# Causal attention with one key head: another order of the query tiles, and part of the second half of the queries computed behind the first shift

## The reference

```python
q = (x @ wq_w.T + wq_b).reshape(b, t, H, HD)        # H = 32, HD = 16, t = 1024
k = (x @ wk_w.T + wk_b).reshape(b, t, HKV, HD)      # HKV = 1
v = (x @ wv_w.T + wv_b).reshape(b, t, HKV, HD)
k1 = k[:, :, 0, :]
v1 = v[:, :, 0, :]
scores = jnp.einsum('bqhd,bkd->bhqk', q, k1) / jnp.sqrt(jnp.float32(HD))
causal = jnp.tril(jnp.ones((t, t), dtype=bool))
scores = jnp.where(causal, scores, -jnp.inf)
weights = jax.nn.softmax(scores, axis=-1)
attn = jnp.einsum('bhqk,bkd->bqhd', weights, v1)
attn = attn.reshape(b, t, H * HD)
return attn @ wo_w.T + wo_b
```

## Time and profile before

| | us |
|---|---|
| median of 3 runs (1402.65 to 1405.58) | 1404.99 |
| profiled execution, its own time | 1405.82 |
| its span, first to last instruction | 1403.9 |
| preparing of the first half of the queries and the keys | 820 to 854.8 |
| maxima of tile 7 with the late events | 854.8 to 905.4 |
| from the last of them to the first score | 905.4 to 911.8 |
| scores, to the last transposes | 911.8 to 1206.3 |

### The profile page before, as it was taken

How to read it: one execution, slowest core, us unless ns; L and a number is a source line. 1 busy time by engine, 2 the same in 40 slices (tenths; PEclk the granted TensorE clock), 3 DMA queues, 4 the chain that set the end, 5 groups by cost and what they waited for, 6 DMA issues and landing times. The chain is left out here.

```text
span 1403.9 us, 14513 instructions
## 1 busy us (share of the span) xinstructions
PE 1288.1 (92%) x5418; PEld 846.5 (60%) x5418; DVE 737.1 (53%) x1283; ACT 429.5 (31%) x718; POOL 162.9 (12%) x211
## 2 busy tenths in 40 slices
PE   7899999599799998987887989899999998799998
PEld 4788666244487787866665434355454443588776
DVE  4322432475666655335576746887776632433264
ACT  2121311211221124221222221166665665312141
POOL 0000000000086100003111240000010123000000
PEclk9999999799899999998898998999999999899999
DMA  8110000840155540005000010000000000122001
GB/s 321 46 45 0 0 0 0 335 152 0 67 203 202 202 179 0 1 0 171 0 1 0 1 45 0 2 0 3 2 2 2 2 3 1 46 82 75 0 23 38
DMA packets 18121, 79.07 MB, mean 56 GB/s; under 512 B 2960, under 2 KB 3600, under 8 KB 15888
## 3 DMA queue, kind: packets, MB, share of 16 engines
q1 hardware_dynamic: 18064, 78.32, 15.3%
HBM read 75.95 MB, written 2.10 MB: 56 GB/s over the span
## 5 line engine op out<-in xcount | busy, mean ns | idle before, releaser
L376 PE MATMUL psum<-L_ffn_x,L_ffn_w_up 128*128 128x512 f32 x1152 | 264.4, 391 | 3.5 <-DVE L_ffn_hidden L505 3.5
L376 PEld LDWEIGHTS psum<-L_ffn_x,L_ffn_w_up 128*128 128x128 f32 x1152 | 217.1, 189 | 50.5 <-DVE L_ffn_hidden L505 5.4
L1817 DVE TENSOR_REDUCE mqa_top<-psum 128x1 f32<-128x512 f32 (+3 forms) x304 | 186.2, 657 | 58.1 <-PE psum L1643 37.7
L1736 ACT ACTIVATE mqa_prob<-psum 128x512 f32<-128x512 f32 x288 | 159.9, 601 | 86.1 <-PE psum L1661 85.0
L393 PE MATMUL psum<-L_ffn_wd,L_ffn_part_h 128*128 128x512 f32 x600 | 142.7, 399 | 7.0 <-DVE L_ffn_wd L301 7.0
L1661 PE MATMUL psum<-mqa_stack,mqa_keys 100*128 100x512 f32 x288 | 133.0, 476 | 4.8 <-DMA mqa_stack<-mqa_rows 3.5
L393 PEld LDWEIGHTS psum<-L_ffn_wd,L_ffn_part_h 128*128 128x128 f32 x600 | 115.0, 193 | 31.9 <-DVE L_ffn_part_h L292 7.8
L1632 PE MATMUL psum<-mqa_keys,mqa_stack 96*128 96x512 f32 (+1 forms) x256 | 108.4, 445 | 1.9 <-DVE mqa_top L1817 1.0
L376 PE MATMUL psum<-L_attn_x,L_attn_w_up 128*128 128x512 f32 x456 | 105.4, 394 | 3.9 <-DVE L_attn_hidden L505 3.9
L376 PEld LDWEIGHTS psum<-L_attn_x,L_attn_w_up 128*128 128x128 f32 x456 | 86.7, 190 | 22.5 <-issue 4.3
L1661 PEld LDWEIGHTS psum<-mqa_stack,mqa_keys 100*128 100x128 f32 x288 | 55.3, 196 | 72.1 <-ACT mqa_prob L1736 62.6
(11 more groups left out here) (246 smaller groups left out, 1699.6 us busy)
## 6 DMA issues: line engine op xcount, KB each, us to landing
L_ffn_stage<-in_L_w SPq DMA_DIRECT2D x25, 768.0 KB, 6.2
L_ffn_z_int<-in_L_z SPq DMA_DIRECT2D x14, 768.0 KB, 4.4
L_ffn_s_all<-in_L_s SPq DMA_DIRECT2D x14, 768.0 KB, 6.2
lora_wo<-in_L_wo SPq DMA_DIRECT2D x8, 1024.0 KB, 9.6
L_attn_stage<-in_L_w SPq DMA_DIRECT2D x10, 512.0 KB, 3.7
L_attn_w_down<-in_L_down SPq DMA_DIRECT2D x1, 2560.0 KB, 24.4
x_feat<-in_x_feat SPq DMA_DIRECT2D x2, 1024.0 KB, 7.1
x_tok<-in_x_tok SPq DMA_DIRECT2D x1, 2048.0 KB, 18.8
```

The costliest lines, as they stand in the source:

```text
L376: ins = nc.tensor.matmul(bank[half][:, :], w_up[:, slot, w_part, at:at + P], x[:, x_part, k, half * HALF:(half + 1) * HALF], start=k == 0 ...
L1736: nc.scalar.activation(prob[:, n % PROBS, :], score_bank[n % 3], ACT.Exp, scale=SCALE)\
L1817: nc.vector.tensor_reduce(top[:, i % 2, lo // HALF, heads[0]:heads[-1] + 1], max_bank[n % 3][:, 0:len(heads) * width] .rearrange("p (h k) ...
```

## The change

Three things in the plan, and what follows from them:

1. The tiles are taken in the order 3, 4, 7, 6, 5, 2, 1, 0. Tile 3 lies in the lower half of the queries, so the lower half is prepared first and the upper one is the late half. The first maxima are the 32 units of tile 3 instead of the 64 of tile 7.
2. Of the 36 late events 23 stand among these 32 units, the other 13 (the last query group, its split and the last 8 spreads) behind `shift_rows` of the first tile and ahead of its first score.
3. Behind each score one unit is taken as before, and so many more that the next tile's units are all taken three steps before the tile's end: 43 units in the 32 steps of tile 3, 64 in the 40 steps of tile 4, 64 in the 64 of tile 7, 56 in the 56 of tile 6, 45 in the 48 of tile 5, none in the last 48 steps (tiles 2, 1, 0), whose plan is that of before, word for word.

```diff
-    order = list(range(NT - 1, -1, -1))
+    order = [3, 4, 7, 6, 5, 2, 1, 0]
...
-    first = len(max_units(0))
+    first, total, in_gap = len(max_units(0)), len(late), 13
     for n in range(first):
         next_max()
-        while late and len(late) > 45 * (first - 1 - n) // first:
+        while len(late) > in_gap + (total - in_gap) * (first - 1 - n) // first:
             plan.append(late.pop(0))
     pending.clear()
     plan.append(("shift_rows", 0))
-
-    ahead = 0
+    plan += late
+
+    units_to = [0]
+    for i in range(NT):
+        units_to.append(units_to[-1] + len(max_units(i)))
     for i, qt in enumerate(order):
-        for n in range(8 * (qt + 1)):
+        steps = 8 * (qt + 1)
+        for n in range(steps):
...
-            for _ in range(2 if i == 0 and n % 5 == 4 else 1):
-                if todo:
+            if todo:
+                next_max()
+            if i + 1 < NT:
+                units = units_to[i + 2] - units_to[i + 1]
+                while n_max < units_to[i + 1] + min(units, -(-(n + 1) * units // (steps - 3))):
                     next_max()
             flush()
...
-                        half, m = 1 - n // KC, n % KC
+                        half, m = n // KC, n % KC
...
+                        if i == 1:
+                            pe.wait_ge(spread_by_act, 16)
+                            pe.wait_ge(spread_by_dve, 16)
```

More of the change, by code:

```diff
@@ L1726, in _ @@
                     elif kind == "spread" and event[1] % 2 == 0:
-                        e, half = event[1], 1 - event[1] // 16
+                        e, half = event[1], event[1] // 16
                         act.wait_ge(spread_ready, e + 1)
```

## The result

The changed kernel takes 1408.58 us (median of 22 runs, 1406.08 to 1411.59), the kernel before beside it 1405.82 us (22 runs). The ratio is 1.0021, with a 95% interval of 1.0011 to 1.0031: slower by 1.5 to 4.4 us. The profiled execution has a span of 1408.6 us. The sum said +5.3 us and 1410, so the way was right and the size about double of the middle of what was measured.

A forecast was written before the change was run, and what follows sets the result against it. PE was taken to bound the score steps, DVE the stretches with many max units and few scores. Terms -16.9 + 8.2 + 14.0 = +5.3 us on 1405.8, taken as 1410 us; 8 in 10 range 1400 to 1419.

The forecast's parts named there:

- The sum: Whole kernel: the three terms together, +5.3 us on the profiled execution's 1405.8; forecast taken as 1410 us.
- First term: Stretch up to the first score: it comes earlier, at 894.9 instead of 911.8, -16.9 us; bounds -19 and -11.
- the clock falls in the first gap too: Rival, first shift into tile 3: filler 3 us longer, three waits 6.8 us low clock each; +11.6, 1416.6 us; chance 0.13.
- Third term: First scores of tiles 4, 7, 6: three new waits for rows, 8.6 us, plus clock 5.4; +14.0, bounds +7 and +19.
- the waits cost only themselves: Rival, behind the three waits for rows: clock stays 1.00, the 5.4 us fall out; -0.1, 1404.9 us; chance 0.23.
- Second term: Score steps get longer: +8.2 us; bounds +2 and +13.
- (c): Score cycles with more than four max units: DVE sets the pace, +4.7 us.
- (b): Behind the first gap: the 6.4 us at clock 0.50 go, -2.9 us.
- The price of DVE's pace: Four-step cycles with more than four units: n units take DVE n x 0.605 + 0.46 us.
- The sign named for it: Steps of tiles 3 and 4: DVE busy for over 95%.
- (a): Score steps: 272 max units instead of 240, the 32 more without mask; +6.4 us.
- The rival of free room on TensorE: Score steps: added maxima cost nothing on TensorE; total -3.3, 1401.7 us; chance 0.18, shared with a shorter prologue.

The follow-up runs named there:

- e1: Changed kernel with the next tile's maxima done seven steps before a tile's end instead of three; 1394.99 us, ratio to the kernel before 0.9926.
- e2: Changed kernel with twelve further matmuls of 512 columns on PE ahead of each of three waits for rows; 1406.03 us, ratio to before 1.0009.
- e3: Changed kernel with all 36 late events among the maxima of tile 3, none behind the first shift; 1409.48 us, ratio to before 1.0027.
- e5: e1 with only the last 4 late events behind the first shift instead of 13; 1390.67 us, ratio to the kernel before 0.9897.
- e7: Changed kernel with the next tile's maxima done five steps before a tile's end instead of three; 1397.52 us, ratio to before 0.9942.
- e8: Changed kernel with the next tile's maxima done four steps before a tile's end instead of three; 1405.49 us, ratio to before 0.9999.
- e4: Kernel before, in its own tile order, with 13 late events put behind the first shift; 1405.74 us, ratio to before 1.0011.

## Why the prediction was right, and where its sizes were off

*First term, -16.9: measured -16.0.* The transposes come 24.1 us earlier (23.6 summed). The filler takes 12.0 us from the transposes to the first score instead of the 10.6 of the sum: its query group runs partly at half clock, 890.72 - 886.24 = 4.5 us instead of 3.1. That was the rival "the clock falls in the first gap too", and it came true in its first half only: it cost 1.4 us of its 3, and tile 3 started at 1.00. That part was luck as well: in e1, with the same seam, tile 3 lost 1.3 us at the low clock.

*Third term, +14.0: measured 13.0* in the changed kernel itself, 8.5 us of waits for rows and 4.5 of clock (e2). The distance between it and e1 from the first score to the end, 13.6, has 1.8 us of waits for DVE's shift in it and lacks e1's own low stretch. The three waits have the size (2.84, 2.80, 2.84 us for 2.9), the place and the releaser that were named; transposes to score is 3.6 rather than 3.9. The clock costs 1.5 us per wait instead of 1.8. Its price was right (1.5 of 3.4 us is 44%, for 45%), the length wasn't: each wait brought 3.4 us, the shortest of the low stretches seen before, and the sum took 4.4. In e3, which has the same three waits, two of the three brought 6.8 us, of which 1.2 and 1.4 lay within the wait. So the length was luck within its bounds.

Is a wait of 2.8 us enough for the clock to fall? The rival "the waits cost only themselves" falls in the profiled executions: in the changed kernel and in e3 the low clock came at all six. But it is no certainty. One wait of 3.40 us in a block that no version touches (L393, the second of rows 7) has a low stretch at it in six of the twelve profiled executions and none in the other six. In e5 it looks like this, timeline and busy time behind it:

```profile
1324.48 10.72 PE L393 MATMUL psum<-L_ffn_wd,L_ffn_part_h 128*128 128x512 f32 x45 [3.40 <-DVE L_ffn_wd L301]
1324.50:1327.90 3.40, 3.40 (x15) 2.84 (x16) 3.40 (x6) 3.40 (x7) 0.00 (x0) 1.00 0.00 0
```

The prediction's "none of this size is without" held for the one trace it was read from. The waits of 0.5 to 1.4 us in e7 and e8 brought none; e1's low stretch shows that the clock can fall behind short ones too.

*Second term, +8.2: measured 7.0* in the changed kernel, the 20.0 us by which everything behind the first score is longer less the 13.0 of the third term; 6.4 and 6.8 in e1 and e5. (The terms of (c) as written add up to 4.5 rather than 4.7, with 2.6 rather than 2.8 for tile 3 to 4.3.) (b) was 2.5 instead of 2.9 (e4). The price of DVE's pace came as the rule said: seven cycles of tile 3 last 27.7 us, against 7 x 3.79 + 1 = 27.5 by it and 7 x 3.41 = 23.9 at PE's pace, and tile 4's last 4.7 without masks against 4.63, and 4.9 to 5.0 with them against 4.74. The sign named for it was wrong: DVE was to be busy for over 95% and is for 26.88 of 31.00 and 40.29 of 46.00 us, 87 and 88%. The rule itself has 0.46 us of idle time in each cycle and so says 88%. In tile 4's masked cycles the two paces lie close, and which of them sets the 4.9 us wasn't told apart.

What the sum left out is the waits for DVE ahead of the later transposes: 4.5 us in the kernel before, 1.8 in the changed one. With these 2.7 us and the 2.5 of (b) the scores' own increase, (a) and (c) together, comes to some 12 us against 11.1 in the sum, an estimate from the idle times. What (a) and (c) each are was not measured apart. So a saving that the prediction did not see made its second term look nearly right.

*The sum.* -16.0 + 13.0 + 7.0 is +4.0 in the traces, against +5.3; the timed runs say +2.8 with 1.5 to 4.4 around it. The changed kernel's profiled execution was 1.9 us slower than the median of its runs, and its mean clock, 0.957, is the lowest value among the 22 (0.957 to 0.962). The mechanism was right in its two large terms; that the total lies so near comes in part of errors of about 1 to 3 us that cancel.

*The rival of free room on TensorE* falls by its length: it left -0.4 us for the second term, and 6.4 to 7.0 were measured. That does not show that it is PE's time that the added units cost, since in the cycles of more than four of them that are shown above DVE's pace is the longer. The Trainium skill (Perfetto Trace Analysis, Identifying the Most-Contended Engine) takes weight-load busy time, beside the share of peak FLOPs, as the measure of headroom. Here weight loads filled 48%, and neither that nor PE's busy time of 100% said what a further unit would cost; the distance of starts, of PE's matmuls and of DVE's reduces, did.

## What to carry to other kernels

When a plan is tightened so that something is ready just in time, count the work that stands in the queue between the request and its first user, in time: here 0.6 us of work for a chain of 3.6 us, three times, ate 13 of the 16 us by which the start was shorter, and four steps more of lead (one number) turned +0.2% into -0.7%. Filler behind a wait pays only up to the wait's own length (4 spreads, not 13 events), and here, by the estimate above, mostly by keeping the clock up; work taken from a stretch that the same engine bounds has not been hidden but moved. And before two plans are compared by a rule per cycle, count the units cycle by cycle: the mean over a tile gave 7 us where the rule itself gives 1 at most.

## What the runs showed that I had not expected

- In the changed kernel three idle times of 2.8 us on PE between dense matmuls were each followed by 3.4 us at about 0.50 of the clock, and twelve matmuls that compute nothing of use kept it at 1.00 in e2's profiled execution. Idle times of 0.5 to 1.4 us in e7 and e8 brought no low clock. Yet the same idle time of 3.40 us (L393) brought one in six executions of twelve, and in e1 the clock fell for 6.8 us where the longest idle time just before was 0.87 us. A single profiled execution doesn't tell how often a wait costs its low clock; the mean clock of the timed runs helps.
- The place of the transposes against the value group matters: e7 to e8, one step, took away the 1.0 us value group between the last maximum and the transposes, and brought 4.9 us of waits for DVE's three small shift instructions.
